# A self-attention, cross-attention and feed-forward block: the score products and the weighted sum moved to the head of TensorE's double step, with the turns, stores and loads one double step apart

## The chip, the core and the metric
One core of a Trainium2 chip runs the whole block. The metric is the device time of one launch in microseconds; smaller is better. The kernel before took 3159.14 us in the median of three runs (3155.99 to 3168.3).

## What is computed
The input x holds 32 sequences of 256 tokens with 256 features, the context 32 sequences of 256 tokens with 192 features, all in fp32. Three blocks follow one another, each with a layer norm ahead and a residual added:

```python
h = _ln(x, g1, be1)
x = _attn(h, h, Wq1, Wk1, Wv1, Wo1, bo1) + x
h = _ln(x, g2, be2)
x = _attn(h, context, Wq2, Wk2, Wv2, Wo2, bo2) + x
h = _ln(x, g3, be3)
y = h @ Wp + bp
a, gate = (y[..., :FF_HID], y[..., FF_HID:])
x = a * gelu(gate) @ W2 + b2 + x
```

`_attn` has 16 heads of 64: q, k, v by projections to 1024 columns, softmax(q k / 8), the weighted sum of v, and the projection by Wo back to 256 columns.

## The kernel before, in words
The program has three stages one after the other: `attention` for self, `attention` for cross, `feed_forward`. The change touches `attention` alone, and so two stages.

**Precision.** Projections and score products take each fp32 operand as a high part (ScalarE copies it to fp32r) and a low part (VectorE or GpSimd subtracts the high part), and add three products. So each result of TensorE in PSUM costs a ScalarE copy and a VectorE subtraction before the next product: `high_parts`/`low_parts` for Q/K, `high_o`/`low_o` for the heads' output, `high_h`/`low_h` for h, `high_context`/`low_context` for the context.

**Pairs and double steps.** Heads go in pairs (8 pairs per sequence). Each engine runs its own `step(b, p, part)` for sequence b and p = 0, 2, 4, 6: a double step of pairs p and p + 1, called step p below. Stages of the pipeline lag behind the projections by a number of pairs: SCORES 1, EXPS 2, NORMED 3, TURNED 4, LOADED 6, WEIGHTED 6, PROJECTED 8. The first sequence is written out, the next 30 are a loop, then come the last sequence and a drain. The order on an engine is the program's order; engines wait for one another by semaphores.

**TensorE, one double step (L758):** `project_qk` (12 matmuls in self, 11 in cross, into the single bank ps_qk), `project_v` (12 or 10), `project_out` twice (6 each), `project_qk` again, in step 2 of cross the transposes of the next context and in step 4 those of the next h (4 matmuls into ps_misc, the bank of v), then `score` twice (12 each, on half the rows of the array, so that two run side by side) and `weigh` twice (8 each).

**A pair's way after the scores.** VectorE takes the maxima of either head (`maxima`, L549), ScalarE the exponentials with their sums (`exps`, L429), VectorE the reciprocals (`inverse`, L576), GpSimd multiplies (`normalise`, L382). To turn the probabilities, VectorE transposes 32x32 blocks (`turn`, L568, into one of two buffers `blocks`), SP stores them to DRAM with four DMAs of 128 KB (`store_turn`, L300) and loads them back in turned order with one of 512 KB (`load_turn`, L308, into a ring of four). `turn` waits until its buffer's last store, that of the pair two before, has landed. Then comes `weigh` (L738), `high_o` (L474), `low_o` (L581), `project_out` (L752), and after eight pairs VectorE adds the residual (`output`, L536).

**SP's queue.** All of these DMAs are issued by SP in program order, on one queue. Per sequence it also loads the next x and context (L282, L271, L272, in step 0), and in step 6, after the turned stores, it stores the output (L292), waits for the landing, and loads the next residual over the old one (L288).

Of the kernel before, what the change touches and what calls it, by code (L numbers as in the profile page):

```python
# [24 lines left out]
F32 = mybir.dt.float32  # L25
# [23 lines left out]
SCORES, EXPS, NORMED, TURNED, LOADED, WEIGHTED, PROJECTED = 1, 2, 3, 4, 6, 6, 8  # L49
# [7 lines left out]
TURN_CONTEXT, TURN_H = 2, 4  # L57
# [10 lines left out]
def sequences(nc, eng, n, step):  # L68


    for p in range(0, PAIRS, 2):
        step(0, p, FIRST)
    with nc.Fori(1, n - 1, engines=[eng.engine], hint_back_edge=True) as b:
        for p in range(0, PAIRS, 2):
            step(b, p, LOOP)
    for p in range(0, PAIRS, 2):
        step(n - 1, p, LAST)
    for p in range(0, PROJECTED, 2):
        step(n, p, DRAIN)

# [59 lines left out]
def attention(nc, tag, x_in, ctx_in, x_out, weights, bo, gamma, beta, prefetch, yout, y_stored, before):  # L140
# [7 lines left out]
    with ExitStack() as es:  # L148
# [110 lines left out]

        def stored_count(b, q):  # L260

            return 16 * QUADS * (PAIRS // 2 * b + q // 2 + 1)
# [4 lines left out]
        def _(sp):  # L267
# [26 lines left out]
            def store_turn(b, p):  # L294

                s = PAIRS * b + p - TURNED
                slot = (p - TURNED) % PAIRS
# [6 lines left out]
            def load_turn(b, p):  # L304

                slot = (p - LOADED) % PAIRS
                sp.wait_ge(turn_stored[slot % 2], stored_count(b, p - LOADED))
# [3 lines left out]
            def step(b, p, part):  # L311
                for pair in (p, p + 1):
                    if alive(part, pair, LOADED):
                        load_turn(b, pair)
                if part in (FIRST, LOOP) and p == 0:
                    load_next(b + 1)
                for pair in (p, p + 1):
                    if alive(part, pair, TURNED):
                        store_turn(b, pair)
                if part == FIRST and p == 2:  # L320
                    prefetch(sp)
                if part in (LOOP, LAST) and p == 6:
                    store(b - 1)
                    sp.wait_ge(y_stored, 16 * b)
                    load_residual(b)
# [9 lines left out]
        def _(pool):  # L335
# [27 lines left out]
            def low_context(b):  # L363
# [3 lines left out]
                pool.tensor_tensor(c_lo[:], c_t[:, 0], c_hi[:, 0].bitcast(F32), ALU.subtract).then_inc(c_ready, 1)  # L367

# [15 lines left out]
            def step(b, p, part):  # L384
                for pair in (p, p + 1):
                    if alive(part, pair, NORMED):
                        normalise(b, pair)
                if part != FIRST and p == 0:
                    residual(b - 1)
                if part in (FIRST, LOOP) and p == 2:  # L390
                    norm_power(b + 1)
                    norm_apply(b + 1)
                if part in (FIRST, LOOP) and p == 6:
                    low_h(b + 1)
                    if cross:
                        low_context(b + 1)
# [14 lines left out]
        def _(act):  # L411
# [71 lines left out]
            def step(b, p, part):  # L483
                g = PAIRS * b + p
                if alive(part, p, PROJECTED):
# [689 lines left out]
```

## Time and profile before
| | |
|---|---|
| median of three runs | 3159.14 us (3155.99 to 3168.3) |
| the profiled execution's own time | 3161.7 us |
| its span, first to last instruction | 3159.9 us |
| mean granted TensorE clock over the span | 0.990 |
| TensorE matmul busy | 2997.0 us (95%) |
| VectorE, ScalarE, GpSimd busy | 2302.1, 1879.8, 1407.4 us |
| DMA moved | 625.01 MB, 198 GB/s over the span |

The self stage runs to about 1282 us and the cross stage to about 2575 us (their last output stores, L292, are issued at 1281.8 and 2575.0); the rest is the feed-forward stage. Times in rows are microseconds from the span's start unless marked ns. A matmul's recorded length includes its way through the array, so the length of a stretch is read from start to start.

### The profile page before, as it was taken

The numbers are of one execution on the slowest core, as the hardware profiler recorded it, in microseconds if no ns is written. First come the engines' busy times: TensorE is split into PE (matmuls) and PEld (weight loads), VectorE is DVE, ScalarE is ACT, GpSimd is POOL, SyncE is SP. The second block draws the span as 40 slices with busy tenths as digits, with TensorE's granted clock in tenths as the row PEclk, the third lists the DMA queues.
The fourth block names the chain that finished last, engine by engine and source line by source line (L and its number), as shares of the span: only waits on it lengthen the run. The fifth ranks groups of instructions, "written<-read, shape, count | busy, mean of one in ns | idle before, by whom it ended". The sixth has DMA issues, their size and how long they took to land. (4 is left out here: it accounts for less than half of the span.)

```text
span 3159.9 us, 77497 instructions
## 1 busy us (share of the span) xinstructions
PE 2997.0 (95%) x25600; PEld 2595.8 (82%) x25600; DVE 2302.1 (73%) x3851; ACT 1879.8 (59%) x5615; POOL 1407.4 (45%) x977
## 2 busy tenths in 40 slices
PE   7999999999999998699999999999999969999999
PEld 6888888888888887588888888888888758888888
DVE  6777777777777776587788777878887755555654
ACT  6666666666666665466666666666666632322232
POOL 5555555555555554455555555555555420001100
PEclk9999999999999999899999999999999989999999
DMA  8777788778787777588888878888888750000000
GB/s 253 235 236 234 233 239 236 233 236 242 237 240 238 236 239 225 173 241 240 239 243 248 240 238 240 242 241 244 240 244 239 229 145 27 27 27 33 33 27 21
DMA packets 464424, 625.01 MB, mean 198 GB/s; under 512 B 57728, under 2 KB 397056, under 8 KB 464128
## 3 DMA queue, kind: packets, MB, share of 16 engines
q1 hardware_dynamic: 460256, 624.09, 66.2%
q10 hardware_dynamic: 4128, 0.41, 0.1%
q8 instruction: 23, 0.38, 0.1%
q14 instruction: 17, 0.14, 0.0%
HBM read 330.71 MB, written 293.60 MB: 198 GB/s over the span
## 5 line engine op out<-in xcount | busy, mean ns | idle before, releaser
L382 POOL TENSOR_TENSOR self_probs<-self_probs,self_row_inv 128x1024 f32<-128x1024 f32 x256 | 484.8, 1894 | 578.2 <-DVE self_row_inv L576 575.4
L382 POOL TENSOR_TENSOR cross_probs<-cross_probs,cross_row_inv 128x1024 f32<-128x1024 f32 x256 | 484.8, 1894 | 565.3 <-DVE cross_row_inv L576 565.3
L429 ACT ACTIVATE cross_probs<-cross_ps_s,cross_neg_max 128x256 f32<-128x256 f32 x1024 | 474.5, 472 | 198.3 <-DVE cross_blocks L568 134.2
L429 ACT ACTIVATE self_probs<-self_ps_s,self_neg_max 128x256 f32<-128x256 f32 x1024 | 474.4, 472 | 121.8 <-DVE self_blocks L568 76.6
L549 DVE TENSOR_REDUCE self_neg_max<-self_ps_s 128x2 f32<-128x512 f32 x512 | 328.8, 684 | 170.2 <-PE self_ps_s L719 170.2
L549 DVE TENSOR_REDUCE cross_neg_max<-cross_ps_s 128x2 f32<-128x512 f32 x512 | 331.6, 684 | 135.0 <-PE cross_ps_s L719 134.0
L568 DVE STREAM_TRANSPOSE cross_blocks<-cross_probs 128x1024 f32<-128x1024 f32 x256 | 315.4, 1232 | 10.3 <-DMA cross_turns<-cross_blocks 9.4
L568 DVE STREAM_TRANSPOSE self_blocks<-self_probs 128x1024 f32<-128x1024 f32 x256 | 315.0, 1231 | 1.0 <-POOL self_probs L382 1.0
L738 PE MATMUL self_ps_o<-self_probs_t,self_v 128*64 128x256 f32 x2048 | 258.3, 388 | 30.4 <-DMA self_probs_t<-self_turns 30.2
L738 PE MATMUL cross_ps_o<-cross_probs_t,cross_v 128*64 128x256 f32 x2048 | 257.7, 389 | 27.2 <-DMA cross_probs_t<-cross_turns 26.8
L481 ACT ACTIVATE self_qk_hi<-self_ps_qk 128x512 fp32r<-128x512 f32 x256 | 153.2, 599 | 213.4 <-PE self_ps_s L719 114.3
L979 ACT ACTIVATE ff_u_hi<-ff_gated 128x512 fp32r<-128x512 f32 x128 | 81.0, 632 | 301.3 <-PE ff_ps_y L1119 214.2
L481 ACT ACTIVATE cross_qk_hi<-cross_ps_qk 128x512 fp32r<-128x512 f32 x256 | 152.7, 596 | 167.4 <-PE cross_ps_qk L656 83.7
L939 POOL TENSOR_TENSOR ff_xres<-ff_xt,ff_b 128x1024 f32<-128x1024 f32 x16 | 38.4, 2401 | 438.0 <-DMA out<-ff_yout 438.0
L738 PEld LDWEIGHTS self_ps_o<-self_probs_t,self_v 128*64 128x64 f32 x2048 | 136.6, 137 | 111.0 <-issue 43.5
L738 PEld LDWEIGHTS cross_ps_o<-cross_probs_t,cross_v 128*64 128x64 f32 x2048 | 136.5, 137 | 107.1 <-issue 40.7
L1063 DVE TENSOR_TENSOR ff_u_lo<-ff_gated,ff_u_hi 128x512 fp32r<-128x512 f32 x128 | 115.4, 901 | 129.2 <-ACT ff_u_hi L979 129.2
L429 ACT ACTIVATION_READ_ACCUMULATOR cross_probs<-cross_ps_s,cross_neg_max 128x1 f32 x1024 | 204.7, 200 | 0.0
L429 ACT ACTIVATION_READ_ACCUMULATOR self_probs<-self_ps_s,self_neg_max 128x1 f32 x1024 | 204.4, 200 | 0.0
L558 DVE TENSOR_TENSOR cross_qk_lo<-cross_ps_qk,cross_qk_hi 128x512 fp32r<-128x512 f32 x256 | 172.2, 672 | 12.1 <-ACT cross_qk_hi L481 7.5
L558 DVE TENSOR_TENSOR self_qk_lo<-self_ps_qk,self_qk_hi 128x512 fp32r<-128x512 f32 x256 | 172.2, 673 | 5.8 <-ACT self_qk_hi L481 5.3
L1046 DVE SCALAR_TENSOR_TENSOR ff_gated<-ff_ps_a,ff_bp,ff_gelu 128x512 f32<-128x512 f32 x128 | 96.0, 750 | 92.9 <-PE ff_ps_a L1092 90.9
(170 smaller groups left out, 9623.8 us busy)
## 6 DMA issues: line engine op xcount, KB each, us to landing
self_turns<-self_blocks SPq DMA_DIRECT2D x1024, 128.0 KB, 2.8
self_probs_t<-self_turns SPq DMA_DIRECT2D x256, 512.0 KB, 4.3
cross_turns<-cross_blocks SPq DMA_DIRECT2D x1024, 128.0 KB, 2.9
cross_probs_t<-cross_turns SPq DMA_DIRECT2D x256, 512.0 KB, 4.3
self_xt<-in_x SPq DMA_DIRECT2D x32, 256.0 KB, 6.3
self_xres<-in_x SPq DMA_DIRECT2D x32, 256.0 KB, 2.7
after_self_attention<-yout SPq DMA_DIRECT2D x32, 256.0 KB, 2.4
cross_xt<-after_self_attention SPq DMA_DIRECT2D x32, 256.0 KB, 6.4
```

Of the source, the lines that this page charges most:

```text
L382: pool.tensor_tensor(tile, tile, scale, ALU.mult).then_inc(probs_ready, 1)
L429: last = act.activation(probs[:, slot % 2, h, t], scores[:, slot % 2, h, t], ACT.Exp, bias=neg_max[:, slot % 2, i:i + 1], accum_out=row_su ...
L481: act.activation(qk_hi[:, p % 2], ps_qk[:], ACT.Copy).then_inc(qk_hi_ready, 1)
L549: nc.vector.tensor_reduce(neg_max[:, slot, r], scores[:, slot, h], AX_X, ALU.max, negate=True).then_inc(neg_max_ready, 1)
L558: nc.vector.tensor_tensor(qk_lo[:, slot], ps_qk[:], qk_hi[:, slot].bitcast(F32), ALU.subtract).then_inc(qk_ready, 1)
L568: nc.vector.transpose(blocks[:, slot].rearrange("p (j a q) -> p a j q", j=QUADS, q=QUAD), probs[:, slot].rearrange("p h t (k j q) -> p (h ...
L738: last = nc.tensor.matmul(ps_o[DHEAD * h:DHEAD * (h + 1), half * SEQ:(half + 1) * SEQ], v[:, k, c:c + DHEAD], turned_t[:, h, k], start=k = ...
L939: pool.tensor_tensor(xres[:], xt[:, parity], bias, ALU.add).then_inc(xres_ready, 1)
L979: act.activation(u_hi[:, slot], gated[:, slot], ACT.Copy).then_inc(u_hi_ready, 1)
L1046: nc.vector.scalar_tensor_tensor(gated[:, slot], ps_a[slot][:], bp_c[:, j:j + 1], gelu[:, slot], ALU.add, ALU.mult).then_inc(gated_ready, 1)
L1063: nc.vector.tensor_tensor(u_lo[:, slot], gated[:, slot], u_hi[:, slot].bitcast(F32), ALU.subtract).then_inc(u_ready, 1)
```

## The change
The lags become SCORES 2, EXPS 2, NORMED 2, TURNED_EVEN 2, TURNED_ODD 4, LOADED 6, WEIGHTED 8, PROJECTED 8, and a sequence's output is added 16 pairs after its first projection. On TensorE a double step begins with both score products and both weighted sums; then come Q/K, v, out, Q/K, out. The transposes of the context and of h stand in v's place in steps 4 and 6, with v at the end. ScalarE copies v, h and the context at the head of its step; GpSimd takes over the lower half of the context's low part from VectorE (L542). SP loads first, then in step 2 stores the output, waits, loads the residual, and then stores the odd and the even pair's turned blocks. The first two sequences are written out, and the drain has one step more. The diff, cut to what does this (`store_turn` and `turn` only get the lag as an argument):

```diff
-SCORES, EXPS, NORMED, TURNED, LOADED, WEIGHTED, PROJECTED = 1, 2, 3, 4, 6, 6, 8
+SCORES, EXPS, NORMED, TURNED_EVEN, TURNED_ODD, LOADED, WEIGHTED, PROJECTED, SUMMED = 2, 2, 2, 2, 4, 6, 8, 8, 16
...
-TURN_CONTEXT, TURN_H = 2, 4
+TURN_CONTEXT, TURN_H = 4, 6
...
 def sequences(nc, eng, n, step):
-    for p in range(0, PAIRS, 2):
-        step(0, p, FIRST)
-    with nc.Fori(1, n - 1, engines=[eng.engine], hint_back_edge=True) as b:
+    for b in range(2):
+        for p in range(0, PAIRS, 2):
+            step(b, p, FIRST)
+    with nc.Fori(2, n - 1, engines=[eng.engine], hint_back_edge=True) as b:
         for p in range(0, PAIRS, 2):
             step(b, p, LOOP)
     for p in range(0, PAIRS, 2):
         step(n - 1, p, LAST)
     for p in range(0, PROJECTED, 2):
         step(n, p, DRAIN)
+    step(n + 1, 0, DRAIN)
...
+        def live(part, b, p, lag):
+            if part == FIRST:
+                return PAIRS * b + p >= lag
+            return PAIRS * (b - n) + p < lag if part == DRAIN else True
...
-            def load_turn(b, p):
+            def load_turn(b, p, part):
                 slot = (p - LOADED) % PAIRS
+                if part == DRAIN:
+                    sp.wait_ge(pv_done, PAIRS * b + p - LOADED - RING + 1)
                 sp.wait_ge(turn_stored[slot % 2], stored_count(b, p - LOADED))
                 sp.dma_start(probs_t[:, slot % RING], turns[slot].rearrange("j k i n -> (j k) (i n)")
                              ).then_inc(turn_loaded[slot % RING], 16)
             def step(b, p, part):
                 for pair in (p, p + 1):
-                    if alive(part, pair, LOADED):
-                        load_turn(b, pair)
+                    if live(part, b, pair, LOADED):
+                        load_turn(b, pair, part)
                 if part in (FIRST, LOOP) and p == 0:
                     load_next(b + 1)
-                for pair in (p, p + 1):
-                    if alive(part, pair, TURNED):
-                        store_turn(b, pair)
-                if part == FIRST and p == 2:
+                if p == 2 and live(part, b, p, SUMMED):
+                    store(b - 2)
+                    sp.wait_ge(y_stored, 16 * (b - 1))
+                    load_residual(b - 1)
+                if live(part, b, p + 1, TURNED_ODD):
+                    store_turn(b, p + 1, TURNED_ODD)
+                if live(part, b, p, TURNED_EVEN):
+                    store_turn(b, p, TURNED_EVEN)
+                if part == FIRST and b == 0 and p == 2:
                     prefetch(sp)
-                if part in (LOOP, LAST) and p == 6:
-                    store(b - 1)
-                    sp.wait_ge(y_stored, 16 * b)
-                    load_residual(b)
...
+                pool.wait_ge(c_ready, 2 * b + 1)
+                pool.tensor_tensor(c_hi[64:P, 1], c_t[64:P, 1], c_hi[64:P, 1].bitcast(F32),
+                                   ALU.subtract).then_inc(c_ready, 1)
+                pool.wait_ge(c_ready, 2 * b + 2)
...
             def step(b, p, part):
-                for pair in (p, p + 1):
-                    if alive(part, pair, NORMED):
-                        normalise(b, pair)
-                if part != FIRST and p == 0:
-                    residual(b - 1)
-                if part in (FIRST, LOOP) and p == 2:
+                if part != DRAIN and p == 0 and counts(b):
+                    low_h(b)
+                    if cross:
+                        low_context(b)
+                if part in (FIRST, LOOP) and p == 4:
                     norm_power(b + 1)
                     norm_apply(b + 1)
-                if part in (FIRST, LOOP) and p == 6:
-                    low_h(b + 1)
-                    if cross:
-                        low_context(b + 1)
+                if p == 6 and live(part, b, p, PROJECTED):
+                    residual(b - 1)
+                for pair in (p, p + 1):
+                    if live(part, b, pair, NORMED):
+                        normalise(b, pair)
...
                 g = PAIRS * b + p
-                if alive(part, p, PROJECTED):
+                even, odd = (p - EXPS) % RING, (p + 1 - EXPS) % RING
+                if p == 0 and counts(b) and part != DRAIN:
+                    high_h(b)
+                    if cross:
+                        high_context(b)
+                elif part != DRAIN and p > 0:
+                    copy_v(b, p - 2)
+                if live(part, b, p, EXPS):
+                    exps(g - EXPS, even, 0)
+                if p == 0 and live(part, b, p, EXPS):
+                    copy_v(b - 1, 6)
+                if live(part, b, p, EXPS):
+                    exps(g - EXPS, even, 1)
+                if live(part, b, p, PROJECTED):
                     high_o(b, p)
                 if part != DRAIN:
                     high_parts(g, p)
-                if alive(part, p, EXPS):
+                if part in (FIRST, LOOP) and p == TURN_H:
+                    scale_shift(b + 1)
+                if live(part, b, p + 1, EXPS):
                     for h in range(2):
-                        exps(g - EXPS, (p - EXPS) % RING, h)
+                        exps(g + 1 - EXPS, odd, h)
                 if part != DRAIN:
-                    copy_v(b, p)
-                    if part in (FIRST, LOOP) and p == TURN_H:
-                        scale_shift(b + 1)
-                    if part in (FIRST, LOOP) and p == 6:
-                        high_h(b + 1)
-                        if cross:
-                            high_context(b + 1)
                     high_parts(g + 1, p + 1)
-                if alive(part, p + 1, EXPS):
-                    for h in range(2):
-                        exps(g + 1 - EXPS, (p + 1 - EXPS) % RING, h)
...
-            def low_context(b):
-                dve.wait_ge(c_hi_ready, b + 1)
-                nc.vector.tensor_tensor(c_hi[64:P, 1], c_t[64:P, 1], c_hi[64:P, 1].bitcast(F32),
-                                        ALU.subtract).then_inc(c_ready, 1)
...
                 g = PAIRS * b + p
-                if alive(part, p, NORMED):
+                if live(part, b, p, SCORES):
+                    for h in range(2):
+                        maxima(g - SCORES, 0, h)
+                if live(part, b, p + 1, TURNED_ODD):
+                    turn(b, p + 1, TURNED_ODD)
+                if live(part, b, p, SCORES):
+                    maxima(g + 1 - SCORES, 1, 0)
                     inverse(b, p)
-                if alive(part, p, PROJECTED):
+                    maxima(g + 1 - SCORES, 1, 1)
+                if p == 0 and live(part, b, p, SUMMED):
+                    output(b - 2)
+                if live(part, b, p, PROJECTED):
                     low_o(b, p)
-                if alive(part, p, TURNED):
-                    turn(b, p)
                 if part != DRAIN:
                     low_parts(g, p)
-                if part != FIRST and p == 6:
-                    output(b - 1)
-                if alive(part, p + 1, TURNED):
-                    turn(b, p + 1)
-                if alive(part, p + 1, NORMED):
+                if part in (FIRST, LOOP) and p == TURN_CONTEXT and cross:
+                    context_copy(b + 1)
+                if live(part, b, p, TURNED_EVEN):
+                    turn(b, p, TURNED_EVEN)
+                if live(part, b, p, SCORES):
                     inverse(b, p + 1)
                 if part in (FIRST, LOOP) and p == 2:
                     norm_stats(b + 1)
-                if alive(part, p, SCORES):
-                    maxima(g - SCORES, (p - SCORES) % 2, 0)
                 if part != DRAIN:
                     low_parts(g + 1, p + 1)
-                if part in (FIRST, LOOP) and p == TURN_CONTEXT and cross:
-                    context_copy(b + 1)
-                if alive(part, p, SCORES):
-                    maxima(g - SCORES, (p - SCORES) % 2, 1)
-                if part in (FIRST, LOOP) and p == 6 and cross:
-                    low_context(b + 1)
-                if alive(part, p + 1, SCORES):
-                    for h in range(2):
-                        maxima(g + 1 - SCORES, (p + 1 - SCORES) % 2, h)
...
             def step(b, p, part):
+                for pair in (p, p + 1):
+                    if live(part, b, pair, SCORES):
+                        score(b, pair)
+                for pair in (p, p + 1):
+                    if live(part, b, pair, WEIGHTED):
+                        weigh(b, pair)
+                context = cross and p == TURN_CONTEXT and part in (FIRST, LOOP)
+                x = p == TURN_H and part in (FIRST, LOOP)
                 if part != DRAIN:
                     project_qk(b, p)
-                    project_v(b, p, part)
-                for pair in (p, p + 1):
-                    if alive(part, pair, PROJECTED):
-                        project_out(b, pair)
+                    if context:
+                        transpose_context(b + 1)
+                    elif x:
+                        transpose_h(b + 1)
+                    else:
+                        project_v(b, p, part)
+                if live(part, b, p, PROJECTED):
+                    project_out(b, p)
+                    if context or x:
+                        project_out(b, p + 1)
                 if part != DRAIN:
                     project_qk(b, p + 1)
-                if part in (FIRST, LOOP) and p == TURN_CONTEXT and cross:
-                    transpose_context(b + 1)
-                if part in (FIRST, LOOP) and p == TURN_H:
-                    transpose_h(b + 1)
-                for pair in (p, p + 1):
-                    if alive(part, pair, SCORES):
-                        score(b, pair)
-                for pair in (p, p + 1):
-                    if alive(part, pair, WEIGHTED):
-                        weigh(b, pair)
+                    if context or x:
+                        project_v(b, p, part)
+                if live(part, b, p, PROJECTED) and not (context or x):
+                    project_out(b, p + 1)
```

## Rows read from the trace of the kernel before

**Rows 1.** The page: busy time of engines; a DMA issue's KB and us to landing.
```profile
PE 2997.0 (95%) x25600; PEld 2595.8 (82%) x25600; DVE 2302.1 (73%) x3851; ACT 1879.8 (59%) x5615; POOL 1407.4 (45%) x977
...
cross_turns<-cross_blocks SPq DMA_DIRECT2D x1024, 128.0 KB, 2.9
```

**Rows 2.** Waits of TensorE: line waited for, us in total, times, longest us.
```profile
PE self_ps_o L738 <- DMA self_probs_t<-self_turns: 30.2, 39, 2.7
PE cross_ps_o L738 <- DMA cross_probs_t<-cross_turns: 26.8, 31, 2.1
```

**Rows 3.** Timeline of TensorE after a wait: start us, us, what [idle before].
```profile
1838.28 0.39 PE L656 MATMUL cross_ps_qk<-cross_c_hi,cross_hi_wk 128*128 128x256 f32 x1 [0.37 <-POOL cross_c_lo L367]
1838.50 0.28 PE L656 MATMUL cross_ps_qk<-cross_c_lo,cross_hi_wk 128*128 128x256 f32 x1
```

**Rows 4.** Instructions on the output tile: ns min/median/max, first and last start.
```profile
L292 SPq MOVE after_self_attention<-yout x30: 29/29/29, 84.4 to 1207.6; - x30
L292 SPq MOVE after_cross_attention<-yout x30: 29/29/29, 1366.8 to 2501.9; - x30
```

**Rows 5.** Timeline of TensorE, self stage: the first score product of four double steps.
```profile
509.04 0.51 PE L719 MATMUL self_ps_s<-self_qk_hi 64*128 64x256 f32 x4
...
518.38 0.51 PE L719 MATMUL self_ps_s<-self_qk_hi 64*128 64x256 f32 x4
...
528.58 0.51 PE L719 MATMUL self_ps_s<-self_qk_hi 64*128 64x256 f32 x4
...
538.36 0.38 PE L719 MATMUL self_ps_s<-self_qk_hi 64*128 64x256 f32 x2
```

**Rows 6.** Timeline of TensorE, cross stage: one undisturbed double step.
```profile
1828.10 0.39 PE L656 MATMUL cross_ps_qk<-cross_h_hi,cross_hi_wq 128*128 128x256 f32 x1
...
1830.65 0.28 PE L752 MATMUL cross_ps_y<-cross_hi_wo,cross_o_hi 128*128 128x256 f32 x1
...
1832.05 0.28 PE L656 MATMUL cross_ps_qk<-cross_h_hi,cross_hi_wq 128*128 128x256 f32 x1
...
1833.18 0.28 PE L656 MATMUL cross_ps_qk<-cross_c_hi,cross_lo_wk 128*128 128x256 f32 x1
1833.39 0.51 PE L719 MATMUL cross_ps_s<-cross_qk_hi 64*128 64x256 f32 x4
...
1836.90 0.39 PE L656 MATMUL cross_ps_qk<-cross_h_hi,cross_hi_wq 128*128 128x256 f32 x1
```

**Rows 7.** Instructions on the context's high part: ns min/median/max, first and last start.
```profile
L542 DVE TENSOR_TENSOR cross_c_hi<-cross_c_t,cross_c_hi x32: 421/1068/1393, 1294.5 to 2502.5; 64x256 fp32r<-64x256 f32 x32
L367 POOL TENSOR_TENSOR cross_c_lo<-cross_c_t,cross_c_hi x32: 725/727/830, 1295.7 to 2503.4; 128x256 fp32r<-128x256 f32 x32
```

**Rows 8.** Timeline of ScalarE and VectorE, cross stage.
```profile
1829.70 0.60 ACT L481 ACTIVATE cross_qk_hi<-cross_ps_qk 128x512 fp32r<-128x512 f32 x1 [0.54 <-PE cross_ps_qk L656]
1829.80 1.23 DVE L568 STREAM_TRANSPOSE cross_blocks<-cross_probs 128x1024 f32<-128x1024 f32 x1
1830.96 0.65 DVE L558 TENSOR_TENSOR cross_qk_lo<-cross_ps_qk,cross_qk_hi 128x512 fp32r<-128x512 f32 x1
...
1837.66 1.29 DVE L549 TENSOR_REDUCE cross_neg_max<-cross_ps_s 128x2 f32<-128x512 f32 x2
```

**Rows 9.** Timeline of SP, cross stage: DMA issues.
```profile
1821.46 3.80 SPq L300 DMA_DIRECT2D cross_turns<-cross_blocks  x8
...
1838.64 0.41 SPq L288 DMA_DIRECT2D cross_xres<-after_self_attention  x1
1839.55 0.81 SPq L308 DMA_DIRECT2D cross_probs_t<-cross_turns  x2
1840.62 0.39 SPq L282 DMA_DIRECT2D cross_xt<-after_self_attention  x1
```

**Rows 10.** Issue to landing: the tile cross_xt; the output store of 1836.07 (KB, us).
```profile
DMA to landing us min/median/max: 2.7/6.4/7.4
...
after_cross_attention<-yout SPq DMA_DIRECT2D x1, 256.0 KB, 2.4
```

More of the change, by code:

```diff
@@ L292, in store, with store_turn @@
                 sp.dma_start(rows(x_out[b]), yout[:]).then_inc(y_stored, 16)
-            def store_turn(b, p):
-                s = PAIRS * b + p - TURNED
-                slot = (p - TURNED) % PAIRS
+            def store_turn(b, p, lag):
+                s = PAIRS * b + p - lag
+                slot = (p - lag) % PAIRS
                 sp.wait_ge(turned, s + 1)
@@ L559, in low_parts, with turn @@
                                         ALU.subtract).then_inc(qk_ready, 1)
-            def turn(b, p):
-                s = PAIRS * b + p - TURNED
-                slot = (p - TURNED) % 2
+            def turn(b, p, lag):
+                s = PAIRS * b + p - lag
+                slot = (p - lag) % 2
                 dve.wait_ge(probs_ready, s + 1)
-                if counts(c := stored_count(b, p - TURNED - 2)):
+                if counts(c := stored_count(b, p - lag - 2)):
                     dve.wait_ge(turn_stored[slot], c)
@@ L620, in _ @@
             for i, w in enumerate(("wq", "wk", "wv")):
-                if w == "wv" and cross:
-                    low_context(0)
                 dve.wait_ge(w_hi_ready, i + 1)
@@ L662, in project_v @@
                     pe.wait_ge(v_ready, c)
-                if cross and part in (FIRST, LOOP) and p == TURN_CONTEXT + 2:
+                if cross and part in (FIRST, LOOP) and p == TURN_CONTEXT:
                     pe.wait_ge(c_t_ready, b + 2)
-                if part in (FIRST, LOOP) and p == TURN_H + 2:
+                if part in (FIRST, LOOP) and p == TURN_H:
                     pe.wait_ge(h_t_ready, b + 2)
@@ L726, in weigh @@
                 q = (p - WEIGHTED) % PAIRS
-                seq = b if p >= WEIGHTED else b - 1
-                pe.wait_ge(v_ready, PAIRS // 2 * seq + q // 2 + 1)
-                if counts(c := PAIRS // 2 * b + (p - WEIGHTED) // 2):
-                    pe.wait_ge(o_ready, c)
+                pe.wait_ge(v_ready, PAIRS // 2 * (b - 1) + q // 2 + 1)
                 slot = (p - WEIGHTED) % RING
```

## The prediction
> **What bounds the kernel now.** I read the page first: TensorE is busy for 95% of the span, VectorE for 73%, and the matrix work of the change is the same instructions in another order, so all that the change can give or take is TensorE's idle time [rows 1]. The waits of TensorE name it: two DMA waits of 30.2 and 26.8 us on the turned probabilities [rows 2], and shorter ones on GpSimd's c_lo [rows 3] and, before the transposes, on ScalarE's copy of v. That view misses what a wait costs afterwards: after a wait of 0.37 us the second matmul came 0.22 us after the first, where 0.12 is the pitch, so each wait costs 0.11 more [rows 3]. So I measured a whole sequence instead. The output store's register instruction comes once in each of 30 sequences: (1207.6 - 84.4)/29 = 38.73 us per sequence in the self stage and (2501.9 - 1366.8)/29 = 39.14 in the cross stage [rows 4]. An undisturbed double step is 9.34 us from score to score in the self stage, and 9.78 with a transpose in it, 0.44 more [rows 5]; in the cross stage it is 1836.90 - 1828.10 = 8.80 us [rows 6]. Clean sequences would take 4 x 9.34 + 0.44 = 37.80 and 4 x 8.80 + 2 x 0.44 = 36.08. **The idle to be had is 0.93 us per sequence in self and 3.06 in cross**, times 31 sequences each: 29 and 95 us. The feed-forward stage isn't touched.
>
> **The change on TensorE.** Before, the order round the loop was scores, weighted sums, Q/K, v, out, out, Q/K. After, it is scores, sums, Q/K, v, out, Q/K, out. The instructions and the switches between tile shapes are the same, so the clean lengths stand. I count time in a double step from its first score product (A; B is 0.82 later), by the cross rows: Q/K at 3.51, out at 6.06, second Q/K at 6.76 with its last matmul ending at 8.17, second out, next score at 8.80 [rows 6]. In self one Q/K and two v matmuls more stand before it, 0.12 us each: out is at 6.42. A transpose group adds 0.44.
>
> **The waits that go.** The turned probabilities are now loaded a whole double step before they are used (lag 6 against 8); what was queued behind two loads had landed 7.5 us after the first of them (below), less than a double step, so both DMA waits go. v's copy moves to the head of ScalarE's step and the transposes stand in v's place, 4 us after it: those waits go. The low parts of h and the context move from late in the last double step of a sequence to the head of the next; behind GpSimd's last normalisation c_lo (0.73 us) is done at about 3.2, and the lower half of c_hi, 1.07 us on VectorE now, follows it there. No row shows that instruction on GpSimd; I take c_lo's 0.73 (as many columns), with VectorE's shortest and longest, 0.42 and 1.39, as the ends [rows 7]. It is done at 4.0 and needed at 4.2: free at 0.73, and 0.5 us per cross sequence (16 us) at 1.39; a gain beyond the wait that it ends is excluded, since TensorE waits for nothing else there. VectorE is relieved of the 1.07, which no wait of TensorE needs.
>
> **The small waits that come.** (1) Score B needs the Q/K product made one matmul group earlier. From the last Q/K matmul's end: ScalarE 0.60, VectorE 0.65, three hops of 0.03 to 0.06 [rows 8], 1.38 us, against 1.33 us of out and score A before B's weight load. Late by 0.05, 0.06 with its restart, in the double steps that end with out: three in self (0.18), two in cross (0.12). (2) VectorE's o_lo stands behind a turn, two maxima and the reciprocal: maximum at 1.02, then starts at 1.62, 2.22 (turn), 3.38, 3.98, 4.07, and o_lo from 4.67 to 5.33, with 0.06 to TensorE 5.39; pitches of 0.60, 1.16 and 0.60 from [rows 8]. Where a transpose stands in v's place, out comes already at 5.35 in cross and 5.46 in self: 0.16 and 0.05 with the restart (its weight load stands 0.12 earlier). In step 0 of cross, v's late copy between the exponentials and the output add delay o_lo to 6.25 against a weight load at 5.93: 0.34.
>
> **The large wait that comes.** SP's order is loads, then in step 2 the output store L292, a wait for its landing, the residual's load, and only then the odd and the even pair's turned stores. Behind that wait on SP is queued everything that turns probabilities. Before, the store stood behind eight small stores; it landed in 2.4 us [rows 10]. Now it stands right behind two 512 KB loads. The row nearest to that is xt, also 256 KB, issued 1.07 us after the first of two loads [rows 9]: 6.4 us to landing in the median (2.7 to 7.4) [rows 10]. I take 7.5 us from the first load's issue to the landing, since the median is of the very order of issue; the ends are 3.0 (2.4 on a free queue, issued 0.6 after the load) and 8.5 (xt's longest).
> Chain in cross: step 0's even turn ends at 8.0, four stores at 0.48 each [rows 9], first load at 10.1, 0.8 into step 2; output landed at 8.3; residual 0.2 later; first odd store 0.91 after that [rows 9] at 9.4; the fourth at 10.8; landed at 13.4 (2.6 later, between 2.4 and 2.9 [rows 10, 1]); that is 4.53 into step 4. There the odd turn reuses that buffer and waits for it, instead of starting at 2.22. VectorE is in order: maximum B, reciprocal, maximum, o_lo follow at the same pitches and TensorE sees o_lo 3.17 after the turn's start, at 7.70. Out was due at 5.35 in that step, since the context's transposes stand before it: 2.35 + 0.11 = **2.46 us per cross sequence**. In self the first load is at 0.7 of step 2 and that step is 9.40 long: turn at 3.9, o_lo at 7.05, out due at 6.42 (no transpose in step 4): 0.63 + 0.11 = **0.74**. The queued even stores land before their turn needs them; score B, the exponentials and GpSimd lie behind the same turn but are due later. Sums: self 0.18 + 0.05 + 0.74 = 0.97 against 0.93; cross 0.12 + 0.34 + 0.16 + 2.46 = 3.08 against 3.06. The change is 31 x (0.04 + 0.02) = +2 us.
>
> **Fill and drain.** A pair's output is projected eight pairs behind its Q/K in both kernels. At each stage's end the last pair's turned stores now stand behind an output store too: first load 9.5 us after the last paired scores, 7.5 to the landing, 0.9 to the stores, 17.9. Before, the same stores went out after two short double steps of turns and loads, at about the same place; I take no difference, and 5 us per stage either way for the range. The sum: 3161.7 (the profiled execution, 2.6 above the median of 3159.1) + 2 = **3164 us**.
>
> The Trainium skill's page "DMA: Bandwidth & Descriptors" (section Anatomy of one DMA) puts a DMA at 2.0 us and its bytes over 436 GB/s, fitted on GpSimd's queue, which makes 2.6 us for this store; the trace agrees with it where the store has the queue free, 2.4, and by it alone the large wait would not be there and the time would be that of the first rival. Its section Queues, rings and completion order says that each DMA engine consumes a ring in its order; the trace agrees, with 6.4 us for xt behind two loads.
>
> **Rivals.** *The round trip is short (faster).* Output and loads overlap and the store lands before 6 in step 2, so that the odd turn is held by nothing. For it: 2.4 us on record, and xt's minimum of 2.7. Against: the median of 31 behind two loads is 6.4. Then only small waits are left, 0.23 in self and 0.62 in cross plus 0.16 in step 4: gains of 0.70 and 2.28, 31 x 2.98 = 92, 3069 us. Each microsecond between gives about 1 us per sequence and stage until self has no more to give. *The round trip is longer (slower).* Step 0's four even stores, 512 KB, are in the queue too, issued just before the loads; before, only a residual load was. If they push the landing back by 1 us, to 8.5 after the first load, both stages pay it in full: 62 us, 3226 us; every bit past 7.5 decides for slower. For it: xt's longest, 7.4 [rows 10]; against: turned stores land in 2.9 in the median [rows 1], so most of them are through by then. That the change doesn't do what it says has no room: the program order is written out.
>
> **Chances.** Forecast, 3140 to 3190: 0.42. Short round trip, 3060 to 3140: 0.30. Long one, 3190 to 3260: 0.28. The range 3080 to 3230 leaves out 0.1 on either side; the likeliest case's own is 3140 to 3190. A measurement of this kernel can tell about 0.5% (16 us) from no change: faster than that 0.32, slower 0.34, within 0.34.
>
> **What would show it.** Right: waits of TensorE on the turned probabilities, v's copy and c_lo near zero; in their place out (L752) waiting for o_lo about 0.5 us in self and 2.3 us in cross, once per sequence; VectorE's turn waiting some 50 to 70 us per stage for the landing of turned stores; SP waiting 5 to 6 us for the output store's landing instead of 2. Wrong: an output store that lands in 3 us; score B waiting for qk_lo by more than 0.1 us; a context transpose or K product that still waits.

## The result, and the profile after
| | median of four runs | span and mean granted clock of the profiled execution |
|---|---|---|
| before | 3158.57 us (3155.99 to 3168.3) | 3159.9 us, 0.990 |
| after | 3230.27 us (3216.43 to 3231.1) | 3214.6 us, 0.976 |

The ratio is 1.021, with a 95% interval of 1.018 to 1.025: slower, where no change was forecast, and at the upper end of the range. The profiled execution is the fastest of the four (3216.43), 54.7 us longer in span than that of before. The other three took some 14 us more, which no row explains; their mean granted clock was 0.973 to 0.974 against 0.976.

First the waits of TensorE, VectorE and SP: line waited for, us in total, times, longest us.
```profile
PE cross_ps_y L757 <- DVE cross_o_lo L595: 70.9, 34, 3.5
...
PE self_ps_y L757 <- DVE self_o_lo L595: 15.9, 25, 2.7
...
PE self_ps_o L743 <- DMA self_probs_t<-self_turns: 5.4, 3, 2.1
...
PE cross_ps_o L743 <- DMA cross_probs_t<-cross_turns: 4.4, 2, 2.5
```
```profile
DVE cross_blocks L582 <- DMA cross_turns<-cross_blocks: 73.3, 31, 4.9
...
DVE self_blocks L582 <- DMA self_turns<-self_blocks: 56.6, 33, 9.3
```
```profile
SPq L296 <- DMA after_self_attention<-yout: 179.2, 31, 6.1
SPq L296 <- DMA after_cross_attention<-yout: 177.7, 31, 6.1
```
The waits of [rows 2] are gone but for the pipeline's filling. In their place stands the one predicted: SP waits 5.8 us for each output store, VectorE's turn about 2.4 us per cross sequence for the stores behind it, TensorE for o_lo. This is the chain in one cross sequence, on SP, VectorE and TensorE (start us, us, what [idle before]); the first score product of step 4 started at 1848.36:
```profile
1840.05 0.86 SPq L318 DMA_DIRECT2D cross_probs_t<-cross_turns  x2
1841.17 0.40 SPq L300 DMA_DIRECT2D after_cross_attention<-yout  x1
1847.70 0.39 SPq L296 DMA_DIRECT2D cross_xres<-after_self_attention  x1
1848.14 4.46 SPq L308 DMA_DIRECT2D cross_turns<-cross_blocks  x8
```
```profile
1853.13 1.25 DVE L582 STREAM_TRANSPOSE cross_blocks<-cross_probs 128x1024 f32<-128x1024 f32 x1 [2.46 <-DMA cross_turns<-cross_blocks]
...
1855.53 0.68 DVE L595 TENSOR_TENSOR cross_o_lo<-cross_ps_o,cross_o_hi 128x512 fp32r<-128x512 f32 x1
```
```profile
1856.26 0.42 PE L757 MATMUL cross_ps_y<-cross_hi_wo,cross_o_hi 128*128 128x256 f32 x1 [2.31 <-DVE cross_o_lo L595]
1856.48 0.41 PE L757 MATMUL cross_ps_y<-cross_hi_wo,cross_o_lo 128*128 128x256 f32 x1
1856.68 0.42 PE L757 MATMUL cross_ps_y<-cross_lo_wo,cross_o_hi 128*128 128x256 f32 x1
1856.90 0.42 PE L757 MATMUL cross_ps_y<-cross_hi_wo,cross_o_hi 128*128 128x256 f32 x1
```
The turn starts 4.77 us into step 4 (4.53 in the prediction), the out product 7.90 (7.70). But the last three rows hold what the prediction left out: these matmuls come 0.20 to 0.22 us apart, not 0.12, and go on so for 3.4 us. The next rows show that stretch, two cross sequences that both have the long wait, and the middle of the cross stage (us, busy us and instructions of PE, PEld, DVE, ACT, POOL, granted clock, DMA share, GB/s):
```profile
1856.50:1859.90 3.40, 3.40 (x18) 3.40 (x18) 2.11 (x4) 0.41 (x2) 1.71 (x2) 0.50 0.81 277
...
1841.20:1882.30 41.10, 38.72 (x346) 33.71 (x348) 29.83 (x52) 26.20 (x85) 22.03 (x16) 0.96 0.79 230
1921.20:1960.40 39.20, 37.05 (x346) 32.05 (x346) 29.70 (x52) 26.07 (x85) 22.03 (x16) 1.00 0.81 240
```
```profile
1450.00:2490.00 1040.00, 984.75 (x8851) 855.97 (x8852) 766.57 (x1310) 672.69 (x2161) 565.93 (x411) 0.97 0.79 233
```
and the same stretch of the kernel before:
```profile
1450.00:2490.00 1040.00, 995.50 (x9134) 850.73 (x9133) 832.55 (x1383) 704.51 (x2233) 565.27 (x401) 1.00 0.81 242
```
The same work takes 41.1 us where the granted clock fell to half (1.2 GHz) for one stretch of 3.4 us right behind the wait, and 39.2 where it did not. Of the 28 cross sequences between the first and the last store below it fell in 19, which took 41.0 us in the mean; the other nine took 39.2 (38.4 to 39.9). Before had no such stretch here. The output store's instructions (xcount, ns, first and last start) give the periods, the time from one sequence's store to the next; the last row is the store's landing:
```profile
L300 SPq MOVE after_self_attention<-yout x29: 29/29/29, 106.8 to 1191.0; - x29
L300 SPq MOVE after_cross_attention<-yout x29: 29/29/29, 1395.6 to 2527.1; - x29
...
DMA to landing us min/median/max: 2.2/6.3/6.6
```
**Where the time went.** Self: (1191.0 - 106.8)/28 = 38.72 us per sequence against 38.73 [rows 4], no change. Cross: 40.41 against 39.14, 1.27 more, some 38 us over 30 sequences. The remaining 17 us of the 54.7 are in the filling and draining of the two stages, 12 of them in self (its last output store is issued at 1293.6 instead of 1281.8).

### The profile page after: what moved, and what is told of

Read it like the earlier page. It is cut to its first block and busy times, and to the rows that moved or that the text cites. A ratio compares the mean times of both kernels' runs of the same rounds, so it can differ in the third digit from the quotient of the medians.

```text
span 3214.6 us, 77753 instructions
## 1 busy us (share of the span) xinstructions
PE 3034.8 (94%) x25600; PEld 2642.6 (82%) x25600; DVE 2245.7 (70%) x3819; ACT 1844.7 (57%) x5615; POOL 1432.9 (45%) x1009
## 5 line engine op out<-in xcount | busy, mean ns | idle before, releaser
L582 DVE STREAM_TRANSPOSE self_blocks<-self_probs 128x1024 f32<-128x1024 f32 x256 | 316.9, 1238 | 71.7 <-DMA self_turns<-self_blocks 56.6
L952 POOL TENSOR_TENSOR ff_xres<-ff_xt,ff_b 128x1024 f32<-128x1024 f32 x16 | 38.5, 2404 | 438.1 <-DMA out<-ff_yout 438.1
L757 PE MATMUL cross_ps_y<-cross_hi_wo,cross_o_hi 128*128 128x256 f32 x512 | 162.5, 317 | 72.9 <-DVE cross_o_lo L595 70.9
L444 ACT ACTIVATION_READ_ACCUMULATOR self_probs<-self_ps_s,self_neg_max 128x1 f32 x1024 | 215.0, 210 | 0.0
L444 ACT ACTIVATION_READ_ACCUMULATOR cross_probs<-cross_ps_s,cross_neg_max 128x1 f32 x1024 | 213.8, 209 | 0.0
```

The source lines that it names most:

```text
L444: last = act.activation(probs[:, slot % 2, h, t], scores[:, slot % 2, h, t], ACT.Exp, bias=neg_max[:, slot % 2, i:i + 1], accum_out=row_su ...
L582: nc.vector.transpose(blocks[:, slot].rearrange("p (j a q) -> p a j q", j=QUADS, q=QUAD), probs[:, slot].rearrange("p h t (k j q) -> p (h ...
L757: last = nc.tensor.matmul(ps_y[:, t * DIM:(t + 1) * DIM], a[:, q % 2, t * P:(t + 1) * P], m[:, q], start=q == 0 and t == 0 and i == 0, sto ...
```

## The experiments
Ratios are to before, with 95% intervals. Periods come from the output store's instruction, 28 intervals each, as above; the self stage, which e4, e8 and e9 don't touch, took 38.74 to 38.89 us in them against 38.72, so 0.1 to 0.2 us of a period is scatter in the kernels that keep the wait.

| kernel | us | ratio | period self, cross |
|---|---|---|---|
| after | 3230.3 | 1.021 (1.018 to 1.025) | 38.72, 40.41 |
| e1_store_last | 3107.8 | 0.987 (0.984 to 0.989) | 38.16, 37.22 |
| e2_prefetch_first | 3207.1 | 1.019 (1.016 to 1.021) | 38.74, 40.53 |
| e3_wait_last | 3090.7 | 0.981 (0.978 to 0.983) | 38.14, 36.99 |
| e4_filled_wait | 3200.6 | 1.015 (1.013 to 1.018) | 38.89, 39.46 |
| e5_best | 3075.6 | 0.975 (0.972 to 0.977) | 38.17, 36.99 |
| e6_store_ahead | 3092.3 | 0.980 (0.977 to 0.982) | 38.16, 36.99 |
| e7_output_head | 3067.1 | 0.972 (0.969 to 0.974) | 38.20, 36.66 |
| e8_wait_short | 3189.3 (one run) | | 38.74, 39.42 |
| e9_wait_long | 3217.0 (one run) | | 38.80, 40.19 |

### The place of the output store and of SP's wait
e1_store_last moves the whole block:
```diff
-                if p == 2 and live(part, b, p, SUMMED):
-                    store(b - 2)
-                    sp.wait_ge(y_stored, 16 * (b - 1))
-                    load_residual(b - 1)
                 if live(part, b, p + 1, TURNED_ODD):
                     store_turn(b, p + 1, TURNED_ODD)
                 if live(part, b, p, TURNED_EVEN):
                     store_turn(b, p, TURNED_EVEN)
...
+                if p == 2 and live(part, b, p, SUMMED):
+                    store(b - 2)
+                    sp.wait_ge(y_stored, 16 * (b - 1))
+                    load_residual(b - 1)
```


> The changed kernel with one edit: in step 2 the output store, SP's wait for its landing and the residual's load stand behind the eight stores of turned probabilities instead of in front of them. Everything else is as in the change, so the matrix work is unchanged. My theory (the turned stores queued behind the output store's landing hold VectorE's odd turn of step 4, that holds o_lo and the out product, and TensorE's clock falls right behind that wait): the wait of TensorE on o_lo goes from 70.9 us in cross and 15.9 in self to under 8 in each, the half-clock stretches inside the cross stage go (some 20 of them, about 2 us each), and the periods fall from 38.72 to 38.0 in self and from 40.41 to 36.7 in cross: 31 x (0.7 + 3.7) = 136 us, 3230 - 136 = about 3095 us (3080 to 3120). Rival 1, the loss is in the new shape of the double step itself (turns between maxima, o_lo late on VectorE): the o_lo wait stays and the cross period stays above 39, time 3190 to 3230. Rival 2, the store is only shifted: the loads of step 4 now stand behind the output store and SP's wait, come late for step 6, and TensorE waits on the turned probabilities instead, one to two us per sequence: 3130 to 3190 us.

Measured 3107.8 us, within my theory's range, though above its 3095. e3_wait_last leaves the store and moves only the wait and the load:
```diff
                 if p == 2 and live(part, b, p, SUMMED):
                     store(b - 2)
-                    sp.wait_ge(y_stored, 16 * (b - 1))
-                    load_residual(b - 1)
...
+                if p == 2 and live(part, b, p, SUMMED):
+                    sp.wait_ge(y_stored, 16 * (b - 1))
+                    load_residual(b - 1)
```


> The changed kernel with one edit: in step 2 the output store stays where it is, in front of the turned stores; only SP's wait for its landing and the residual's load stand behind them. It tells the waiting of the issuing engine from the place in the queue. If it is SP's wait that holds the turned stores, they are issued at once, at about 2 us into step 2 instead of 9, and are only behind 1.3 MB of earlier transfers in the queue: the odd turn of step 4 is held by nothing, the o_lo wait falls below 8 us per stage and the time is that of the kernel with the whole block moved, about 3095 us (3080 to 3120). Rival (the queue itself is what is slow: the turned stores would land as late whoever waits): the stores are issued early but still land 4 us into step 4, SP's wait for the output landing goes but the o_lo wait stays above 40 us in cross, time 3190 to 3230.

Measured 3090.7 us. SP of this kernel in the same place of a sequence, and the landing of its output stores:
```profile
1855.97 0.87 SPq L318 DMA_DIRECT2D cross_probs_t<-cross_turns  x2
1857.10 0.40 SPq L300 DMA_DIRECT2D after_cross_attention<-yout  x1
1858.75 5.95 SPq L308 DMA_DIRECT2D cross_turns<-cross_blocks  x8
1864.97 0.41 SPq L296 DMA_DIRECT2D cross_xres<-after_self_attention  x1
```
```profile
DMA to landing us min/median/max: 2.2/6.4/7.2
```
The store is as slow as in the change, 6.4 us, and nobody pays for it, since SP comes to its wait when the store has landed: the turned stores are issued 1.65 us behind it instead of 7. So the waiting of SP was the cost, not the transfer.

e6_store_ahead keeps the wait where it is and puts `store(b - 2)` in front of the step's two loads:
```diff
             def step(b, p, part):
+                if p == 2 and live(part, b, p, SUMMED):
+                    store(b - 2)
                 for pair in (p, p + 1):
...
                 if p == 2 and live(part, b, p, SUMMED):
-                    store(b - 2)
                     sp.wait_ge(y_stored, 16 * (b - 1))
```


> The changed kernel with one edit: in step 2 the output store goes out in front of the two loads of turned probabilities instead of behind them; SP still waits for its landing, and loads the residual, in front of the turned stores. It tests the size of the wait from the other side: not by letting nobody wait, but by giving the store another place in the queue. My theory (the store takes 6.3 us only because two 512 KB loads stand in front of it, and 2.2 to 2.4 us on a free queue): issued right behind the small stores of step 0, its landing falls to 3 to 4.5 us, most of which passes while SP waits for those stores anyway; SP's own wait for it falls from 5.8 us to under 1.5 per sequence, the odd turn is held by nothing, and the time is that of e3_wait_last within 15 us: 3080 to 3105 us. Rival (the landing is slow because of all the traffic around, not because of the place): landing stays above 5.5 us, SP waits 3 us or more, and the time is 3120 to 3200 us.

Measured 3092.3 us. Its SP waits, and the landing of its output stores:
```profile
SPq L296 <- DMA after_cross_attention<-yout: 33.6, 31, 1.4
SPq L296 <- DMA after_self_attention<-yout: 33.0, 31, 1.3
```
```profile
DMA to landing us min/median/max: 2.2/2.6/3.1
```
The landing falls from 6.3 to 2.6 us by the place alone: two 512 KB loads in front of it on the same queue were the 3.7 us. Either half of the fault mended gives all of it back. In e1 the store lands in 2.3 us too, but SP waits there in front of the next step's loads and stores (57.6 us in cross); its cross period is 0.23 longer than that of e3 and e6. It isn't the mechanism of its rival 2: TensorE waits 2.9 us in all of cross for turned probabilities, but 12.9 us, 15 times, for o_lo (7.6 us, 4 times, in e3), and VectorE's turn 12.5 us, 13 times, for turned stores (4.8, once, in e3).

### The clock behind the wait
e4_filled_wait doesn't touch the wait's cause; it fills the wait with matmuls whose results are computed again anyway:
```diff
                 if part != DRAIN:
-                    project_qk(b, p)
+                    project_qk(b, p, 1 if context else 0)
                     if context:
-                        transpose_context(b + 1)
+                        transpose_context(b + 1, 2)
```


> The changed kernel with more matrix work, whose results are overwritten: in the cross stage, in the one double step of each sequence in which TensorE waits 2.3 us for o_lo, the first pair's Q/K product is computed twice and the context's transposes three times before they are signalled, some 2.2 us of matmuls in the place of the wait. The wait's cause isn't touched. It tests the clock. My theory (the granted clock falls to half after the wait, for one stretch of 3.4 us, in some 20 or more of the 30 cross sequences, and costs about 2 us in each): the wait on o_lo shrinks to a fifth or so, no half-clock stretch is left inside the cross stage, and its period falls from 40.41 or more to 39.0 to 39.3, although more work is done: 3230 - 30 to 45 = about 3190 us (3180 to 3205). Rival (the clock has nothing to do with the wait, or the extra work delays what follows): the half-clock stretches stay and the time is 3225 to 3260.

Measured 3200.6 us, and 39.46 us per sequence: more work in less time, by 0.95 us per sequence. e8 and e9 (one run each) leave part of the wait (`project_qk(b, p, 1 ...)` with the transposes once; the Q/K product once with `transpose_context(b + 1, 1)`):

> The kernel of e4_filled_wait with half the filling: the first pair's Q/K product is computed twice in the waiting double step of the cross stage, 11 matmuls at 0.12 us, and the transposes once. TensorE's wait on o_lo should be 2.3 - 1.3 = 1.0 us instead of nearly nothing. If any wait of this place costs the clock, the half-clock stretches of the cross stage stay at 20 or so and the period near 40.4; if only the long one does, as 25 waits of 0.6 us in the self stage without a half-clock stretch suggest, they go, the period is 39.0 to 39.5 us, and the time lies near that of e4_filled_wait, 3195 to 3210 us.

> The same with little filling: only the context's transposes are computed twice, 4 matmuls at 0.11 us, which leaves a wait of about 1.9 us of the 2.3. If the clock falls by the wait's length in steps, some 10 to 25 half-clock stretches stay in the cross stage and the period is 39.8 to 40.8 us; if the fall needs the whole 2.3 us, none stays and the period is 39.0 to 39.3 us.

The middle of the cross stage of e4, e8 and e9, columns as above (the granted clock stands third from the end):
```profile
1450.00:2490.00 1040.00, 1035.20 (x9574) 905.34 (x9574) 783.95 (x1342) 685.05 (x2206) 582.73 (x424) 1.00 0.80 239
```
```profile
1450.00:2490.00 1040.00, 1014.28 (x9355) 882.75 (x9355) 785.19 (x1343) 687.98 (x2217) 580.31 (x421) 1.00 0.80 240
```
```profile
1450.00:2490.00 1040.00, 991.93 (x9001) 863.18 (x9000) 772.25 (x1320) 676.83 (x2174) 568.61 (x412) 0.98 0.79 235
```
Here a wait is counted from one matmul's start to the next. With the wait filled, or cut to 0.5 to 1.5 us, no half-clock stretch is left in the 28 sequences; with 1.3 to 2.4 us there are 13 of them, with the full wait (1.5 to 2.9) 19. The wait causes the fall. In e8 the mean wait is 1.3 us shorter than in the change (1.14 against 2.42) and the work 1.3 us longer, and still a sequence is 0.99 us shorter: that is the clock.

The price of one fall is less than 41.0 - 39.2 = 1.8 us, because the sequences with a fall also had the longer waits (2.53 against 2.19 us in the mean). Less its wait, a sequence took 38.5 us with a fall and 37.0 without, and in e9 39.0 and 37.4: a fall costs 1.5 us. Over all sequences, 19/28 x 1.5 = 1.0 us, the 0.99 of e8. Two sequences with like waits, 2.3 us, can differ in whether the clock falls; why is open.

### The filling
In the change SP's loads of the next stage's weights stand between the first turned stores and the next ones. SP in the first sequence of the change:
```profile
29.84 1.78 SPq L308 DMA_DIRECT2D self_turns<-self_blocks  x4
31.67 0.46 SPq L125 DMA_DIRECT2D raw<-in_L_xattn_Wq  x1
...
35.74 0.59 SPq L125 DMA_DIRECT2D raw<-in_L_xattn_Wo  x1
36.38 8.50 SPq L308 DMA_DIRECT2D self_turns<-self_blocks  x8
44.92 0.44 SPq L318 DMA_DIRECT2D self_probs_t<-self_turns  x1
```
e2_prefetch_first puts them ahead:
```diff
+                if part == FIRST and b == 0 and p == 2:
+                    prefetch(sp)
                 if live(part, b, p + 1, TURNED_ODD):
                     store_turn(b, p + 1, TURNED_ODD)
                 if live(part, b, p, TURNED_EVEN):
                     store_turn(b, p, TURNED_EVEN)
-                if part == FIRST and b == 0 and p == 2:
-                    prefetch(sp)
```


> The changed kernel with one edit: in step 2 of sequence 0 of each stage SP issues the loads of the next stage's weights in front of the first stores of turned probabilities, instead of behind the first and ahead of the later ones. It acts once per stage. My theory (the first-sequences loss of 18.9 us in self and 13.4 in cross is the 4 MB of weight loads standing in the queue in front of the turned loads that the first weighted sums need): the first two sequences get 8 to 15 us shorter in self and somewhat less in cross, the later sequences keep their 38.72 and 40.41; time 3230 - 20 = about 3210 us (3200 to 3220). Rival (the fill is longer because the probabilities are now used two pairs later, so the pipe takes a double step more to fill): unchanged within 4 us, 3226 to 3234.

```profile
29.47 10.09 SPq L308 DMA_DIRECT2D self_turns<-self_blocks  x12
39.60 0.94 SPq L318 DMA_DIRECT2D self_probs_t<-self_turns  x2
```
Measured 3207.1 us. The first turned load goes out at 39.60 instead of 44.92, and the last of the weights has landed at 31.48 instead of 47.68. The self stage's first output store in the loop comes at 95.1 instead of 106.8, and from the last one in self to the first in cross it is 95.1 us instead of 102.0: 11.7 + 6.9 = 18.6 us, about the 17 us in filling and draining. (The span of e2 is only 11.1 us shorter, since its cross sequences took 0.12 us more, with 20 falls of the clock instead of 19, and the stages' ends some us; the medians differ by 23. Between e3 and e5 below, whose cross sequences are alike, the same edit takes 16.2 us off the span.) A wait of TensorE of 10.7 us on qk_lo in the first sequence, and a half-clock stretch of 13.7 us behind it, are gone with it.

### Together


> The kernel of e3_wait_last with the edit of e2_prefetch_first as well: SP's wait for the output store's landing and the residual's load stand behind the turned stores, and in the first sequence the next stage's weight loads go out in front of the first turned stores. Both losses have been shown apart: 3090.7 us with the first alone, and 23 us less than the change with the second alone by medians (11 by profiled spans). If they are independent, as one acts once per sequence and the other once per stage, the time is 3091 - 11 to 23 = 3068 to 3080 us, 0.973 to 0.977 of before, and the first output store of the self stage goes out near 95 us instead of 108. Rival (the fill that is saved is taken back by the first sequence's other waits): 3085 to 3092 us.

Measured 3075.6 us. The gains of e3 and e2 add within the scatter of the runs: 125.2 and 11.1 us of the profiled spans apart, 141.4 together; 139.6 and 23.2 us of the medians, 154.7 together.

e7_output_head takes up one small term. In e3, VectorE in step 0 of a cross sequence (first score product at 1846.07):
```profile
1847.09 1.29 DVE L564 TENSOR_REDUCE cross_neg_max<-cross_ps_s 128x2 f32<-128x512 f32 x2 [0.78 <-PE cross_ps_s L728]
...
1851.02 0.68 DVE L557 TENSOR_TENSOR yout<-cross_ps_y,cross_xres 128x512 f32<-128x512 f32 x1
1851.62 0.68 DVE L596 TENSOR_TENSOR cross_o_lo<-cross_ps_o,cross_o_hi 128x512 fp32r<-128x512 f32 x1
```
The output sum stands right ahead of o_lo, while the engine idles 0.78 us at the step's head.
```diff
+                if p == 0 and live(part, b, p, SUMMED):
+                    output(b - 2)
                 if live(part, b, p, SCORES):
                     for h in range(2):
                         maxima(g - SCORES, 0, h)
...
-                if p == 0 and live(part, b, p, SUMMED):
-                    output(b - 2)
```


> The kernel of e5_best with one more edit: in step 0 VectorE makes the output sum at the head of its step, ahead of the first maximum, instead of between the maxima and o_lo. It tests the 0.34 us that I had put on o_lo in step 0 of the cross stage. In e3_wait_last VectorE is idle for some 0.8 us ahead of the first maximum of that step, and o_lo ends at 6.2 us into it, 0.35 late for the out product. If the output sum (0.68 us) moves there, the first maximum starts about 0.3 later and o_lo ends about 0.3 earlier: 0.3 x 31 = 9 us less in cross and nothing in self, 3059 to 3071 us. Rival (the delayed maxima delay the exponentials and the chain behind them as much): no difference from e5_best within 4 us, or some us slower.

Measured 3067.1 us, 8.5 less than e5; the cross period falls by 0.33, and in the middle of the cross stage step 0 takes 8.86 to 8.90 us, where e3 has 9.19. This is the fastest version, 2.8% below the kernel before (0.969 to 0.974).

## Why the prediction was right in its range and wrong in its sum
**The forecast was no change, +2 us by the sum; the median rose by 71.7 us, and the profiled execution was 54.7 us longer in span.** Two terms of the sum failed, the cost behind the large wait and the filling. That the range reached the result, at its very end, is luck: its upper part stood for another mechanism. Step by step:

- *The waits that go* went, all three. GpSimd's instruction for the context's low part, which no row of before showed, took 0.73 us, the value chosen.
- *The large wait that comes* was right in mechanism and, within 0.12 us of the mean, in size: the output landed 7.47 us after the first load's issue (1840.05 to 1847.52; 7.5 taken), the turn at 4.77, out at 7.90, a wait of 2.31. The row of xt, also queued behind two loads [rows 10], was the right neighbour to take it from. In self the period stayed at 38.72, where the sum had 37.80 + 0.97 = 38.77.
- *What the wait costs afterwards* is the step that failed. I took the 0.11 us of restart seen after a wait of 0.37 us [rows 3] and carried it over to a wait six times as long. In its place: the granted clock falls to half for 3.4 us behind most waits of this length, 1.5 us each. The sum had 36.08 + 3.08 = 39.16 us for a cross sequence; the mean was 40.41. Of the 1.25 between them the clock is 1.0, some 31 us over the stage; the rest is a wait 0.12 longer than the sum's (the change waits 2.42 us in the mean and is 2.4 longer than e3 without the clock, where the sum had 2.46 - 0.16 = 2.30) and small waits 0.13 longer (below). So it is partly chance that the nine sequences without a fall took just 39.2: their waits were shorter than the mean. In its loops before had one wait above 2.0 us (2.04, counted from matmul to matmul) and no half-clock stretch, which fits. But its trace had a row of this length, the longest wait of [rows 2], in the last sequence of self, with the clock of the 3.4 us behind it:
```profile
1218.90 1.08 PE L738 MATMUL self_ps_o<-self_probs_t,self_v 128*64 128x256 f32 x8 [2.73 <-DMA self_probs_t<-self_turns]
```
```profile
1220.50:1223.90 3.40, 3.40 (x17) 2.52 (x14) 1.29 (x2) 0.60 (x1) 0.21 (x1) 0.50 0.63 212
```
  I had read the clock of the span, 0.990, and did not ask what the new wait would do to it.
- *Fill and drain* was the second: "no difference, 5 us per stage" considered only the last pairs. The 17 us are about what the place of the weight loads costs (16.2 from e3 to e5). The diff leaves them at the end of step 2 of the first sequence; but turned stores now begin in that step and no longer in step 4 (TURNED 4 became TURNED_EVEN 2), so that the loads stand in the middle of them. I had followed SP's order in the loop and not in the first sequence.
- *The small waits* held nearly. With the large wait gone, e3 shows what is left: in step 0 of cross o_lo ended at 6.23 us (6.25 predicted), and a sequence took 38.14 us in self against 37.80 + 0.23 = 38.03, and 36.99 in cross against 36.08 + 0.62 + 0.16 = 36.86. Its four cross steps took 9.19, 8.97, 9.42 and 9.41 us, where the sum has 9.20, 8.86, 9.40 and 9.40: most of the 0.13 is in step 2 and is not traced further.
- *The rivals.* The long round trip's number, 3226, was met, but not by its mechanism: the landing did not come later than 7.5. The short one, 3069 us without the wait, is what e3 is but for the filling (3090.7), and e5 with the filling mended (3075.6). So the balance of gains against losses was read rightly, and the change contains a gain of 2% that one wait in SP's program hid.

The Trainium skill's page "DMA: Bandwidth & Descriptors" (section Anatomy of one DMA) gives 2.0 us plus the bytes over 436 GB/s, fitted on GpSimd's queue; the estimate from it for this store is 2.6 us. e6 measured 2.6 where the queue in front is free of loads, the change 6.3 where it is not.

## What to carry to other kernels
Where one engine issues all DMAs in order, look at what stands behind each wait for a landing; move the wait behind the issues that somebody needs, or the waited transfer ahead of the large ones, and if either is done the other doesn't matter. When a change gathers several short waits of TensorE into one long one, price the granted clock behind it too, from a row that shows a wait of that length; the trace of before may hold one outside the loop, as it did here. Follow a reordered queue through the first sequence as well as through the loop.

## What the runs showed of the hardware
Filling an idle stretch of TensorE with useless matmuls made the kernel faster: 1.3 us of them per sequence took 0.99 us off each (e8), since the granted clock stayed at 2.4 GHz instead of falling to 1.2 for 3.4 us. The waits that it follows are short: in the loops of the cross stage falls came behind 2.0 to 2.9 us from one matmul's start to the next, though not behind every wait of that length, and none behind the 28 of 0.5 to 1.5 us in e8, in this kernel's pattern of load. One fall cost 1.5 us. Of a 256 KB store on SP's queue the runs show 2.6 us to landing behind small stores (e6) and 6.3 us right behind two 512 KB loads (the change).
